# A macaron transformer of two layers: L0 FFN without the LN a block ahead, and a third PSUM bank in the expert down projection

## The reference

```python
# layer 0
x = x + 0.5 * L0_ffn(layernorm(x))
x = x + L0_attn(layernorm(x))          # RWKV time mix
x = x + 0.5 * L0_ffn(layernorm(x))
# layer 1
x = x + 0.5 * L1_ffn(layernorm(x))
x = x + L1_attn(layernorm(x))          # linear attention + 3-tap convolution
x = x + 0.5 * L1_ffn(layernorm(x))

def L0_ffn(x):                          # x_prev: x shifted by one token, 0 first
    xr = mu_r * x + (1 - mu_r) * x_prev
    xk = mu_k * x + (1 - mu_k) * x_prev
    return sigmoid(xr @ W_r.T) * (square(relu(xk @ W_k.T)) @ W_v.T)

def L1_ffn(x):                          # 8 experts, top 2, and a shared one; FFN/2 = 1536
    out = sum over e of comb[:, e] * ((silu(x @ wg[e].T) * (x @ wu[e].T)) @ w_down[e].T)
    return shared(x) + out              # shared: the same form with its own weights
```

## Time and profile before

| | us |
|---|---|
| timed runs | 8289.73 and 8750.67, median 8520.2 |
| the profiled execution | 8284.86 |
| its span, slowest core (core 3) | 8283.8 |
| spans of all cores | 8216.5 to 8283.8 |

### The profile page before, as it was taken

How to read it: one execution, slowest core, us unless ns; L and a number is a source line. 1 busy time by engine, 2 the same in 40 slices (tenths; PEclk the granted TensorE clock), 3 DMA queues, 4 the chain that set the end, 5 groups by cost and what they waited for, 6 DMA issues and landing times.

```text
span 8283.8 us, 76057 instructions; the slowest of 8 cores (8216.5 to 8283.8 us)
## 1 busy us (share of the span) xinstructions
PE 5829.2 (70%) x26720; PEld 2634.2 (32%) x26720; DVE 2030.3 (25%) x3690; ACT 1571.0 (19%) x2695; POOL 560.1 (7%) x679
## 2 busy tenths in 40 slices
PE   4543347396988888887981547296978988987993
PEld 1232223142333333333430123142333333433331
DVE  3355654101111111111112451101111111111111
ACT  1133232121111111111111330121111111111110
POOL 0000000000100101001100000000010011001000
PEclk8766678697999999999996858698999999999996
DMA  4401042415445435525325013515255255255234
GB/s 92 97 6 39 23 92 64 94 59 97 67 68 85 73 56 89 83 43 92 61 44 147 11 49 82 102 58 102 45 87 85 45 85 87 46 82 90 45 64 127
DMA packets 352004, 592.34 MB, mean 72 GB/s; under 512 B 17784, under 2 KB 152952, under 8 KB 351632
## 3 DMA queue, kind: packets, MB, share of 16 engines
q0 software_dynamic: 191024, 377.56, 29.9%
q1 hardware_dynamic: 160608, 209.91, 8.0%
HBM read 604.23 MB, written 209.72 MB: 98 GB/s over the span
## 4 chain that ended last, share of the span: by engine, by line
PE 51%; DMA 29%; DVE 8%; ACT 6%; issue 5%; another core or an unknown queue 1%; DVEq 0%; ACTq 0%; POOLq 0%; POOL 0%; SPq 0%
DMA l1f_acc<-arena 20%; PE pb L1304 18%; PE pb L1312 18%; PE pb L1338 4%; PE pb L403 3%; PE pb L575 2%; PE pb L1049 2%; PE pb L424 1%; DMA arena<-l1f_acc 1%; DVE arena L1088 1%; ACT arena L1092 1%; PE pb L1095 1%; DVE arena L562 1%; DMA arena<-xC 1%
## 5 line engine op out<-in xcount | busy, mean ns | idle before, releaser
L1338 PE MATMUL pb<-arena 128*128 128x512 bf16 x6912 | 1570.4, 385 | 501.6 <-ACT arena L1346 500.9
L1304 PE MATMUL pb<-arena 128*128 128x512 bf16 x6912 | 1659.8, 384 | 111.0 <-ACT arena L1321 74.8
L1312 PE MATMUL pb<-arena 128*128 128x512 bf16 x6912 | 1646.6, 381 | 39.3 <-DMA arena<-l1f_wu 39.3
L1324 DVE TENSOR_TENSOR arena<-pb,arena 128x512 bf16<-128x512 f32 x768 | 531.1, 692 | 3861.2 <-PE pb L1312 2256.4
L1338 PEld LDWEIGHTS pb<-arena 128*128 128x128 bf16 x6912 | 671.1, 99 | 1388.6 <-issue 639.1
L1304 PEld LDWEIGHTS pb<-arena 128*128 128x128 bf16 x6912 | 671.8, 98 | 955.5 <-issue 180.9
L1312 PEld LDWEIGHTS pb<-arena 128*128 128x128 bf16 x6912 | 680.8, 99 | 870.9 <-issue 67.5
L1321 ACT ACTIVATE arena<-pb 128x512 bf16<-128x512 f32 x864 | 517.3, 599 | 2113.6 <-PE pb L1304 2081.5
L1348 POOL DMA_DIRECT2D l1f_acc<-arena x576 | 469.4, 815 | 4940.3 <-ACT arena L1346 2920.6
L1346 ACT COPY arena<-pb 128x512 f32<-128x512 f32 x576 | 337.7, 586 | 2179.5 <-DMA l1f_acc<-arena 1492.1
L1330 DVE TENSOR_TENSOR arena<-arena 128x512 bf16<-128x512 bf16 x864 | 367.6, 425 | 528.9 <-PE pb L1304 326.1
(11 more groups left out here) (165 smaller groups left out, 2546.4 us busy)
## 6 DMA issues: line engine op xcount, KB each, us to landing
l1f_acc<-arena POOLq DMA_DIRECT2D x576, 256.0 KB, 3.9
arena<-l1f_yd SPq DMA_DIRECT2D x72, 1024.0 KB
arena<-l1f_wd POOLq DMA_DIRECT2D x16, 3072.0 KB, 23.9
arena<-l1f_wg POOLq DMA_DIRECT2D x16, 3072.0 KB, 43.4
arena<-l1f_wu POOLq DMA_DIRECT2D x16, 3072.0 KB, 61.7
arena<-l1f_acc SPq DMA_DIRECT2D x8, 2048.0 KB
arena<-x_in SPq DMA_DIRECT2D x4, 2048.0 KB
xA<-arena SPq DMA_DIRECT2D x4, 2048.0 KB, 7.1
```

Source lines behind the costliest of these rows:

```text
L1304: P.pe(lambda nc, h=h, mt=mt, pg=pg, wg=wg, ys=ys: nc.tensor.matmul(pg.ap, wg.ap[:, h, mt * 128:(mt + 1) * 128], ys.ap[:, h, :], start=(h ...
L1312: P.pe(lambda nc, h=h, mt=mt, pu=pu, wu=wu, ys=ys: nc.tensor.matmul(pu.ap, wu.ap[:, h, mt * 128:(mt + 1) * 128], ys.ap[:, h, :], start=(h ...
L1324: P.dve(lambda nc, pu=pu, su=su, cr=cr: nc.vector.tensor_tensor(su.ap, pu.ap, cr.ap, op=ALU.mult), [pu.r(), cr.r()], [su.r()])
L1338: P.pe(lambda nc, hk=hk, dh=dh, pd=pd: nc.tensor.matmul(pd.ap, s_wd.ap[:, hk, dh * 128:(dh + 1) * 128], s_h.ap[:, hk, :], start=(hk == 0), ...
```

## The change

In `emit_l0ffn` the two functions `ln_mix` and `mm_out` become one loop body: block b's loads, LN, mixes, matmuls and store are recorded before anything of block b+1. `s_xr` and `s_xk` have one buffer each instead of two, and `s_d` is float32 instead of bf16. The `x`, `y` and `xbf` buffers stay double. In `emit_l1ffn` the down phase's groups go in turn into psum 4, 7 and 2 by `dh % 3`, instead of into 4 and 7. No operation is added or removed.

```diff
--- before.py
+++ after.py
@@ -343,9 +343,9 @@
     s_m2 = A.alloc("l0f_m2", [128, TB], F32)
     s_rstd = A.alloc("l0f_rstd", [128, TB], F32)
     s_mbf = A.alloc("l0f_mbf", [128, 2 * TB], BF16)
-    s_xr = [A.alloc(f"l0f_xr{i}", [128, CH, TB], BF16) for i in range(2)]
-    s_xk = [A.alloc(f"l0f_xk{i}", [128, CH, TB], BF16) for i in range(2)]
-    s_d = A.alloc("l0f_d", [128, CH, TB], BF16)
+    s_xr = A.alloc("l0f_xr", [128, CH, TB], BF16)
+    s_xk = A.alloc("l0f_xk", [128, CH, TB], BF16)
+    s_d = A.alloc("l0f_d", [128, CH, TB], F32)
     s_sr = A.alloc("l0f_sr", [128, CH, TB], BF16)
     s_ka = A.alloc("l0f_ka", [128, CH, TB], BF16)
     s_t = A.alloc("l0f_t", [128, TB], F32)
@@ -353,12 +353,11 @@
     xin_v = x_in.rearrange("(h p) t -> p h t", p=128)
     xout_v = x_out.rearrange("(h p) t -> p h t", p=128)
 
-    def ln_mix(b):
+    for b in range(NB):
         xb = s_x[b % 2]
         yb = s_y[b % 2]
         yprev = s_y[(b + 1) % 2]
         xbf = s_xbf[b % 2]
-        xr, xk = s_xr[b % 2], s_xk[b % 2]
         t0 = b * TB
         P.dma('SYNC', 'xin', lambda nc, xb=xb, t0=t0: nc.sync.dma_start(
             out=xb.ap, in_=xin_v[:, :, t0:t0 + TB]),
@@ -381,22 +380,17 @@
             s_d.ap, ycur, ysh, op=ALU.subtract),
             [yb.r()], [s_d.r()])
         for h in range(CH):
-            P.dve(lambda nc, h=h, yb=yb, xr=xr: nc.vector.scalar_tensor_tensor(
-                xr.ap[:, h, :], s_d.ap[:, h, :], mu_sb.ap[:, 0, h:h + 1],
+            P.dve(lambda nc, h=h, yb=yb: nc.vector.scalar_tensor_tensor(
+                s_xr.ap[:, h, :], s_d.ap[:, h, :], mu_sb.ap[:, 0, h:h + 1],
                 yb.ap[:, h, 1:TB + 1], op0=ALU.mult, op1=ALU.add),
-                [s_d.r(b0=h * TB * 2, b1=(h + 1) * TB * 2), mu_sb.r(), yb.r()],
-                [xr.r(b0=h * TB * 2, b1=(h + 1) * TB * 2)])
-            P.dve(lambda nc, h=h, yb=yb, xk=xk: nc.vector.scalar_tensor_tensor(
-                xk.ap[:, h, :], s_d.ap[:, h, :], mu_sb.ap[:, 1, h:h + 1],
+                [s_d.r(b0=h * TB * 4, b1=(h + 1) * TB * 4), mu_sb.r(), yb.r()],
+                [s_xr.r(b0=h * TB * 2, b1=(h + 1) * TB * 2)])
+            P.dve(lambda nc, h=h, yb=yb: nc.vector.scalar_tensor_tensor(
+                s_xk.ap[:, h, :], s_d.ap[:, h, :], mu_sb.ap[:, 1, h:h + 1],
                 yb.ap[:, h, 1:TB + 1], op0=ALU.mult, op1=ALU.add),
-                [s_d.r(b0=h * TB * 2, b1=(h + 1) * TB * 2), mu_sb.r(), yb.r()],
-                [xk.r(b0=h * TB * 2, b1=(h + 1) * TB * 2)])
-
-    def mm_out(b):
-        xb = s_x[b % 2]
-        t0 = b * TB
-        for (wbf, src, dst, bank0) in ((wr_bf, s_xr[b % 2], s_sr, 2),
-                                       (wk_bf, s_xk[b % 2], s_ka, 4)):
+                [s_d.r(b0=h * TB * 4, b1=(h + 1) * TB * 4), mu_sb.r(), yb.r()],
+                [s_xk.r(b0=h * TB * 2, b1=(h + 1) * TB * 2)])
+        for (wbf, src, dst, bank0) in ((wr_bf, s_xr, s_sr, 2), (wk_bf, s_xk, s_ka, 4)):
             for dh in range(CH):
                 pb = psum[bank0 + dh % 2] if bank0 == 2 else (psum[4] if dh % 2 == 0 else psum[7])
                 for h in range(CH):
@@ -439,12 +433,6 @@
         P.dma('SYNC', 'xout', lambda nc, xb=xb, t0=t0: nc.sync.dma_start(
             out=xout_v[:, :, t0:t0 + TB], in_=xb.ap),
             [xb.r()], [dram_reg(x_out, t0, t0 + TB)])
-
-    ln_mix(0)
-    for b in range(NB):
-        if b + 1 < NB:
-            ln_mix(b + 1)
-        mm_out(b)
     A.release()
 
 
@@ -1332,8 +1320,9 @@
                     [sg.r(), su.r()],
                     [s_h.r(b0=mt * TB * 2, b1=(mt + 1) * TB * 2)])
             for dg in range(4):
-                for (di, pd) in ((0, psum[4]), (1, psum[7])):
+                for di in range(2):
                     dh = dg * 2 + di
+                    pd = (psum[4], psum[7], psum[2])[dh % 3]
                     for hk in range(HK):
                         P.pe(lambda nc, hk=hk, dh=dh, pd=pd: nc.tensor.matmul(
                             pd.ap, s_wd.ap[:, hk, dh * 128:(dh + 1) * 128],
```

## The result

| | before | after |
|---|---|---|
| profiled execution, us | 8284.86 | 8563.19 |
| its cores, us | 8216.5 to 8283.8 | 8485.0 to 8562.1 |
| mean granted clock of its cores | 0.865 to 0.871 | 0.818 to 0.840 |
| lowest timed run, us | 8261.58 | 8452.16 |

The ratio after to before is 1.026, with a 95% interval of 1.018 to 1.034. Set on the profiled execution of before that is 8284.9 x 1.0259 = 8499.5 us, 5 us beyond the top of the forecast's range (8495), and slower by more than 2% where 1.9% was forecast. All times compared here leave out executions in which a whole die ran at a lower clock, since both kernels have these; 5 of the changed kernel's 13 are left, and these are what is counted.

A forecast was written before the change was run, and what follows sets the result against it. TensorE was taken to bound most of the kernel, a DMA chain the down phase of each expert body. 8284.9 + 138 (L0 FFN) + 20 (third bank) gave 8443 us, range 8395 to 8495.

The forecast's parts named there:

- L0 FFN term: Both L0 FFN calls: each block runs its normalising and mixing, then its matmuls, uncovered; +138 us, bounds +121 to +155.
- LN phase: L0 FFN block, from the first L1076 to the last `s_xr` slice: 37.8 us, no longer covered by matmuls.
- matmul phase: L0 FFN block, L403 matmuls after the mixes, then L424: 47.3 us, with 2.1 us for a slow clock.
- third bank's mechanism: Expert down phase: copies stay bound by DMAs, TensorE's pauses become one of 6.0 us, slow matmuls follow; +20 us, bounds 0 and +36.
- cover of 1.5 us: Expert bodies: TensorE's wait for the Silu hides 1.5 of 2.1 us lost to slow matmuls, so 0.6 us shows.
- L1294's wait: Sign in the expert bodies: TensorE's wait ahead of L1294 grows to about 6 us each, some 360 in all.
- L1338's: Sign in the expert down phase: TensorE's waits ahead of L1338 fall by some 150 us, a body keeps 70 us.
- from the sum to the slowest core: Whole kernel: the summed terms, 8443 us, taken as the measured time, with about 0.2% for spread between runs.
- Rival 1: Expert down phase: the 603.0 us of waits ahead of L1338 and L1294 vanish, giving 7820 us; chance 0.03.
- Rival 2: Expert bodies: the bank gives one turn, about 1.7 us less in 60 bodies, giving 8321 us; chance 0.05.
- Rival 3: Expert bodies: the pooled pause costs 2.1 us in 60 bodies, uncovered, 126 us, giving 8549 us; chance 0.10.
- Rivals 4 and 5: L0 FFN: slow clock lasts through L403 groups, 8635 us, chance 0.04; or the mix hides after all, 8305 us, chance 0.02.

The follow-up runs named there:

- e6_serial_bf16: L0 FFN part of the change alone, with `s_d` kept in bf16, two banks as before, against the kernel before: ratio 1.015 (1.010 to 1.020).
- r_after: The changed kernel run again without an edit, beside the kernel before on chip 4: ratio 1.022 (1.013 to 1.032).
- r_before: The kernel before run again without an edit, for a profile on chip 4: ratio 1.000 (0.997 to 1.003).
- e4_ab8: The kernel before with eight `s_ab` buffers instead of two, two banks as before: ratio 0.908 (0.899 to 0.916), fastest run 7544.6 us.
- e8_after_ab8: The changed kernel, both parts, with eight `s_ab` buffers instead of two: 7687.8 us in a single run.
- e5_bank_pz1: The kernel before with the third bank alone, and L1294 writing psum 1 instead of psum 4: 8464.6 us in a single run.
- e1_bank_only: The kernel before with the third bank in the expert down phase alone: ratio 1.002 (0.996 to 1.008).
- r_serial: The kernel before with the L0 FFN part of the change alone, two banks as before, second trial: ratio 1.016 (1.011 to 1.020).

## Why the prediction was wrong, point by point

**The L0 FFN term held.** The LN phase was put at 37.8 us and takes 37.6, the matmul phase at 47.3 and takes 47.3, the calls at 341.6 and 338.9 and take 341.1 and 340.0. The clock loss behind the mixes was put at 2.1 us (its row gives 7.24 - 5.21 = 2.0) and is 28.55 - 121 x 0.217 = 2.3. The float32 difference was put at 2.1 us more and is 2.12. What the forecast did not see is that the longer L380 also cost TensorE: with bf16 its matmuls of one block were 1.1 us shorter (`e6_serial_bf16`).

**The third bank's mechanism held, its size was low.** The copies stayed on the DMA chain, L1282 kept its release, and the pooled pause is 6.36 us where 6.0 was worked out. 20 us were forecast with 0 to 36 as bounds. Cores 6 and 7 of the profiled execution, which kept their clock best in the L1 FFN calls, have 2853 and 2749 us there, 22 and 16 more than the medians of before: 37 us, at the upper bound. On chip 4 `r_after` has 12 us more than `r_before` in the medians of the calls and 26 in the bodies, and 0.7 us in the median body; on chip 6 the median body has 0.5 us more. That is some 12 to 43 us. Two steps of the term were low. It took half of the bodies as slow already; in truth 26% were on the first chip, and 97% are with the third bank. And it took a cover of 1.5 us in each of 60 bodies, where the earlier trace rows has it 49 times: 60 x 2.1 - 74.8 = 51 us and not 36 for the upper bound. The cover itself was real, and it is used up: the wait for the Silu is 4.9 us on core 6 now, 76.3 before.

**The waits.** L1294's wait was to rise to some 360 us; on cores that kept their clock it reads 358.8 (core 0) and 363.6 (core 6), on the slowest core 303.6, where slower down matmuls eat into the pause. L1338's was to fall by 150 us and fell by 204 on core 6 (450.1 to 246.6) and by 193 on core 0 (465.7 to 272.5): the small waits went, 172 waits on core 6 became 34, and the 12 stalls of over 10 us among them are left as they were, 220 us in sum before and 222 after. The body got no shorter all the same.

**The step that failed is the last one, from the sum to the slowest core.** With 139 and 37 us the sum gives 8284.9 + 176 = 8461 us. The ratio over all counted runs says 8499.5, another 38 us. The forecast gave 0.2% for spread between runs, and it kept the chance for slower at 0.41 because the sum stood just under 2%. The median core bears the sum out. In the lowest run of the changed kernel, 8452.2 us, its span is 8439 us against 8257 in the profile of before, 182 more, and on chip 4 the counted runs of the two kernels have 8489 and 8313 on average, 176 more. What comes on top are the stretches at a lower clock on a pair of cores. In three of the five counted runs of the changed kernel the slowest pair stands 38, 79 and 103 us over the median core (8563, 8512 and 8557 us), in the other two the slowest core 12 and 32. The slowest core of the profiled execution has such a stretch in its second L1 FFN call, worth 2869 - 2750 = 119 us there, with 2750 for the cores that kept their clock. One such stretch on one pair lifts the metric, and no term of the forecast had it.

Whether the change makes them more frequent was not settled. The kernel before has them too: its ten counted runs on chip 6 have the slowest core 6 to 59 us over the median one, 38 on average, against 53 for the five of the changed kernel. The level of 0.81 is in both profiles of the changed kernel (all cores; cores 0 to 3) and in neither of the two of the kernel before, nor in those with one part alone; but it is in `e4_ab8`, with the L0 FFN of before (cores 4 to 7), not in `e8_after_ab8`, which has both parts, and for 9 us on two cores in `e5_bank_pz1`. One profile of each kernel can't tell a rate. With the ratio of the second trial, 8470 us, the forecast's range would have held, so part of the miss may be the draw of the five counted runs. The sum of the parts alone (1.016 and 1.002, together 1.018) lies in the second interval, 1.013 to 1.032, and at the lower edge of the first, 1.018 to 1.034.

**The rivals.** Rival 1, the waits vanish, needed another cause, and `e4_ab8` shows it: they go with six more `s_ab` buffers. Rival 2, one turn gained, is out by `e1_bank_only` and `e5_bank_pz1`. Rival 3, the slow clock uncovered, is real but not in this kernel; `e5_bank_pz1` has it. Rivals 4 and 5 are out by the timeline of the L0 FFN.

## What to carry to other kernels

When an engine waits for a bank, look at what the reader of that bank waits for. Here the copies waited for a DMA, so a third bank only moved the pauses, and six more buffers on the other side of the copy took them away. And when small pauses are pooled into one, ask what the clock does behind it and whether a wait is left there to take up the slow matmuls.

In an in-order program, a stage that starts with a long chain on other engines costs TensorE the whole chain unless the matmuls of the block before are issued behind it: here 70 us a call for four blocks, of which 56 are the order and the rest the float32 difference (`e6_serial_bf16`).

## What the runs showed of the hardware

- A pause of 6.4 us was followed by 8 matmuls in 3.6 us instead of 1.9, in 97% to 100% of the bodies (`after`, `e1_bank_only`), while pauses of 0.2 to 2.1 us with matmuls between them were followed by slow ones in 26% to 38% (`before`, `r_before`, `r_serial`). Filling the long one with matmuls for nothing kept the clock up and made the bodies 0.5 us shorter.
- A scalar-tensor-tensor operation of 128x512 takes 0.75 us with a bf16 or a float32 first operand, while a float32 output makes the plain tensor-tensor difference of 128x4096 take 4.42 us instead of 2.30.
- Pairs of neighbouring cores run for hundreds of us at a granted clock of about 0.8 with dense matmuls, beside other cores that do not (core 5 at 0.80 and core 0 at 0.91 from 7200 to 7800 us, cores 6 and 7 at 371 us and the others at 341 to 343 in the first L0 FFN call). Of one die, cores 4 and 5 spend 1550 us at 0.81 and cores 6 and 7 730.
- An accumulate DMA of 256 KB into DRAM holds a stream that waits for its own predecessor to one every 4.4 to 4.8 us (`after`; 4.6 to 5.3 in the earlier trace rows), while the plain writes of the shared expert, of the same size, go out every 2.8 us (`before`, from 1725.80 us on). Eight source buffers instead of two hid that behind the next body's matmuls and took 9% off the kernel (0.908).
